# Where the value writes of a context projection stand in the DMA queue, and the last chunk's in two pieces

## The chip, the cores and the metric

The kernel runs on one core of one Trainium2 chip. The metric is device time in microseconds (us). Engines are named as the profile names them: PE is TensorE, DVE VectorE, ACT ScalarE, POOL GpSimd, SP SyncE, which here only issues DMAs and waits.

## What is computed

The reference is a four-layer Perceiver block stack. 128 latent tokens of width 256 attend, in each layer, to one context of 12544 tokens of width 192, with 16 heads of 16; then self-attention of some kind and a mixture of experts follow. Cut to what matters here:

```python
for l in range(4):
    x = x + cross_attention(layernorm(x), ctx_768, ...)   # q = x Wq; k = ctx Wk + bk; v = ctx Wv
    x = x + self_attention(layernorm(x))
    x = x + experts(layernorm(x))
```

The keys and values of layers 0, 1 and 2 depend on the context alone. They are computed once, in a first stage, and kept in DRAM.

## The kernel before

The stage in question is `project_context` (L190 to L397). Everything else in the kernel comes after it, behind a barrier of all engines, and is not touched.

The context comes transposed (192 x 12544) and is cut into 7 chunks of 1792 keys (`NCH`, `CH`), and each chunk into 2 halves of 896 (`W`), so 14 halves, i = 0 to 13. In half i the kernel makes, for 3 layers and 2 groups of 128 columns, six key tiles (n = 0 to 5), and seven value tiles (t = 0 to 6) of 128 keys x 768 columns.

- PE: `key_tile` (L273) and `value_tile` (L283) take turns, n = 0 to 5, then a seventh value tile. Both have two pairs of PSUM banks. A key tile waits until DVE has taken the key tile before the last, a value tile likewise (`values`).
- ACT: for each key tile `high` (L304) makes the first bf16 part, with a wait for the landing of the part six tiles back (`RING` = 6, semaphores `parts_out`), and `middle` (L311) the second part of the tile before. At the end of half i comes `round_context(i + 2)` (L315), which waits for the load of half i+2 (`ctx`).
- DVE: `key_rest` (L362) and `take_value` (L372) in turns, and at the half's end `low_context(i + 2)`. `take_value` copies a value tile into one of two buffers `values[c % 2]`, 128 x 48 x 14 x 17 fp32 (3 layers x 16 heads, 14 tiles of 128 keys, 16 values and a one). With the first tile of a chunk c it waits for the value writes of chunk c-2 (`values_out`).
- POOL: the third bf16 part of each key tile (L395, semaphore `low`).
- SP: all DMAs go out from one written order (L227 to L269). For each half and each n it waits for `low` and writes the three parts of the key tile (L255, 672 KB); behind n = 1 it issues `load(i + 2)` (L228: one DMA of 448 KB and two of 224 KB). Behind n = 5 of every odd half it waits for the chunk's 14 value tiles and issues three value writes, one for each layer (L265, 1904 KB each, in rows of 14 x 17 x 4 = 952 bytes). At the end SP waits for all landings, and the stage ends.

Of the kernel before, what the change touches and what calls it, by code (L numbers as in the profile page):

```python
# [38 lines left out]
H = 16  # L39
# [5 lines left out]
NCH = NK // CH  # L45
TPC = CH // 128
SUB = CH // 4
GT = TPC // 2
GW = GT * 128
VW = HD + 1  # L50
# [6 lines left out]
class Stage:  # L57
# [5 lines left out]
    def sem(self, name):  # L63
        if name not in self.sems:
            self.sems[name] = self.nc.alloc_semaphore(f"{self.tag}_{name}")
        return self.sems[name]
# [37 lines left out]
def dram(ap, offset, pattern):  # L104

    return bass.AP(ap.tensor, offset, pattern)
# [83 lines left out]
def project_context(nc, g, a):  # L190

    NL = 3
    W = CH // 2
    NH = 2 * NCH
# [3 lines left out]
    with ExitStack() as ctx:  # L198
        st = Stage(nc, ctx, "proj")
        sem = st.sem  # L200
# [11 lines left out]
        values = [st.sb(f"values{i}", [128, NL * H, TPC, VW]) for i in range(2)]  # L212
# [13 lines left out]
        @block.sync  # L226
        def _(sp):  # L227
            def load(i):  # L228
                keys = slice(i * W, i * W + W)
                if i >= 2:  # L230
                    sp.wait_ge(sem("split"), 2 * (i - 1))
                sp.dma_start(raw_a[i % 2][:], a["ctxT"][0:128, keys]).then_inc(sem(f"ctx{i % 2}"), 16)
                for copy in range(2):
                    sp.dma_start(raw_b[i % 2][copy * C1:copy * C1 + C1, :], a["ctxT"][128:C, keys])\
                      .then_inc(sem(f"ctx{i % 2}"), 16)

            for l in range(NL):
                cols = slice(l * D, l * D + D)
                for w, name in ((0, "Wk"), (1, "Wv")):
                    src = a[f"L{l}_xattn_{name}"]  # L240
                    sp.dma_start(w_a[:, w, cols], src[0:128, :]).then_inc(sem("weights"), 16)
                    for copy in range(2):
                        sp.dma_start(w_b[copy * C1:copy * C1 + C1, w, cols], src[128:C, :]).then_inc(sem("weights"), 16)
                if l > 0:
                    for k in range(DG):
                        sp.dma_start(bk[:, l, k:k + 1], dram(a[f"L{l}_xattn_bk"], 128 * k, [[1, 128], [1, 1]]))\
                          .then_inc(sem("weights"), 16)
            load(0)
            load(1)
            for i in range(NH):  # L250
                for n in range(NK2):
                    l, k, u = n // DG, n % DG, i * NK2 + n
                    sp.wait_ge(sem("low"), u + 1)
                    dst = dram(g.key_parts, ((l * 3) * D + k * 128) * NK + i * W, [[NK, 128], [D * NK, 3], [1, W]])
                    sp.dma_start(dst, parts[u % RING][:]).then_inc(sem(f"parts_out{u % RING}"), 16)  # L255
                    if n == 1 and i + 2 < NH:
                        load(i + 2)
                if i % 2 == 1:
                    c = i // 2
                    sp.wait_ge(sem("values"), TPC * (c + 1))  # L260
                    for l in range(NL):
                        dst = dram(g.values, l * g.layer_values + c * 128 * TPC * VW,
                                   [[TPC * VW, 128], [NCH * 128 * TPC * VW, H], [1, TPC * VW]])
                        src = values[c % 2][:, l * H:l * H + H, :, :].rearrange("p h t e -> p h (t e)")
                        sp.dma_start(dst, src).then_inc(sem(f"values_out{c % 2}"), 16)  # L265
            for r in range(RING):
                sp.wait_ge(sem(f"parts_out{r}"), 16 * len(range(r, NH * NK2, RING)))
            for r in range(2):
                sp.wait_ge(sem(f"values_out{r}"), 16 * NL * len(range(r, NCH, 2)))  # L269

        @block.tensor
        def _(pe):
# [2603 lines left out]
```

## Time and profile before

| | us |
|---|---|
| median of 3 runs | 3386.88 |
| the runs | 3374.2 to 3387.84 |
| the profiled execution | 3375.52 |
| its span | 3373.8 |
| the projection, start to last landing of its DMAs | about 467 |
| PE busy in the span | 2941.7 (87%) |
| value writes in the projection | 21, 1904 KB each, 17.4 us from issue to landing (median) |
| writes of key parts | 84, 672 KB each, 4.1 us (median) |

The profile is one execution. Its times count from the span's start. "SPq" is SP's sequencer issuing a DMA: the number there is the time that the issue took, not the transfer. A landing is counted from the start of the issue.

### The profile page before, as it was taken

What the parts mean: (1) busy time and instruction counts of PE and PEld (TensorE: products, weight loads), DVE (VectorE), ACT (ScalarE), POOL (GpSimd) and SP (SyncE); (2) the same over time, 40 slices, a digit from 0 to 9 for tenths busy, and PEclk for the clock granted to TensorE, in tenths of its full rate; (3) what the DMA queues carried; (4) which work ended last, traced back from release to release, by engine and by line L of the source; (5) the groups of instructions that cost most, each with busy time, mean ns of one, the idle gap of its engine ahead of it and who ended that gap; (6) DMA issues with size and microseconds to landing.
All of it is one profiled execution on the core that took longest, in us unless ns stands there. A gap on an engine that the chain in (4) does not pass through costs nothing. (4 is left out here: it accounts for less than half of the span.)

```text
span 3373.8 us, 66493 instructions
## 1 busy us (share of the span) xinstructions
PE 2941.7 (87%) x27158; PEld 2484.3 (74%) x27158; DVE 1829.3 (54%) x3246; ACT 1349.5 (40%) x2191; POOL 405.4 (12%) x571
## 2 busy tenths in 40 slices
PE   6878829998677999576999669999999999999978
PEld 6878725776474777473777455999999999999867
DVE  5445427774426775455776343555555555555524
ACT  4444314666003667122667120444344344444311
POOL 2333310000100000000000002220202020200000
PEclk9989968999787999686999685999999999999969
DMA  4877868883468884059885271201101010000016
GB/s 154 266 259 253 274 190 184 177 175 62 154 192 179 174 177 88 26 204 181 177 175 103 83 213 38 57 11 29 39 1 39 1 39 1 1 1 1 17 50 227
DMA packets 244901, 393.95 MB, mean 117 GB/s; under 512 B 33491, under 2 KB 207957, under 8 KB 244597
## 3 DMA queue, kind: packets, MB, share of 16 engines
q1 hardware_dynamic: 244599, 389.70, 44.9%
q8 instruction: 217, 3.56, 0.5%
q14 instruction: 85, 0.69, 0.1%
HBM read 289.45 MB, written 99.49 MB: 115 GB/s over the span
## 5 line engine op out<-in xcount | busy, mean ns | idle before, releaser
L697 DVE TENSOR_REDUCE L_xattn_tops<-psum 128x1 f32<-128x896 f32 x672 | 702.1, 1086 | 264.8 <-PE psum L549 263.6
L610 ACT ACTIVATE L_xattn_probs<-psum 128x512 f32<-128x512 f32 x1176 | 612.0, 600 | 489.4 <-PE psum L560 489.3
L1705 DVE TENSOR_TENSOR L_units_low<-psum,L_units_high 128x896 fp32r<-128x896 f32 x224 | 243.6, 1088 | 486.7 <-ACT L_units_high L1654 486.7
L549 PE MATMUL psum<-L_xattn_keys,L_xattn_q_stack 96*128 96x448 bf16 (+1 forms) x1344 | 393.6, 377 | 109.0 <-DMA L_xattn_q_stack<-query_parts 64.5
L1622 PE MATMUL psum<-wide_tokens,L_units_high 128*128 128x386 f32 x1568 | 456.4, 358 | 1.4 <-DVE L_units_low L1705 1.4
L560 PEld LDWEIGHTS psum<-L_xattn_q_stack,L_xattn_keys 99*128 99x128 bf16 (+1 forms) x4704 | 321.4, 98 | 143.3 <-issue 17.4
L560 PE MATMUL psum<-L_xattn_q_stack,L_xattn_keys 99*128 99x128 bf16 (+1 forms) x4704 | 392.4, 221 | 5.0 <-ACT L_xattn_probs L610 5.0
L1623 PE MATMUL psum<-wide_tokens,L_units_low 128*128 128x194 f32 x1568 | 395.1, 252 | 0.0
L573 PE MATMUL psum<-L_xattn_probs,L_xattn_values 128*17 128x128 f32 x9408 | 357.1, 276 | 0.0
L1654 ACT CAST L_units_high<-psum 128x896 fp32r<-128x896 f32 x224 | 203.3, 908 | 363.6 <-PE psum L1610 363.6
L1646 ACT ACTIVATE L_units_raw<-L_units_raw,L_units_negmax 128x896 f32<-128x896 f32 x224 | 221.6, 1037 | 307.9 <-DVE L_units_negmax L1696 307.9
L1623 PEld LDWEIGHTS psum<-wide_tokens,L_units_low 128*128 128x128 f32 x1568 | 299.1, 191 | 1.7
L1622 PEld LDWEIGHTS psum<-wide_tokens,L_units_high 128*128 128x128 f32 x1568 | 294.9, 188 | 3.0 <-DVE L_units_low L1705 1.6
L573 PEld LDWEIGHTS psum<-L_xattn_probs,L_xattn_values 128*17 128x17 f32 x9408 | 260.1, 98 | 38.0 <-ACT L_xattn_probs L610 0.6
L1686 DVE TENSOR_SCALAR_CACHE_REDUCE L_units_raw<-psum 128x448 f32<-128x448 f32 x448 | 259.8, 617 | 4.0 <-POOL wide_acc L1665 2.6
L549 PEld LDWEIGHTS psum<-L_xattn_keys,L_xattn_q_stack 96*128 96x128 bf16 (+1 forms) x1344 | 91.4, 99 | 219.1 <-issue 67.1
L1610 PE MATMUL psum<-band,L_units_raw 128*128 128x128 f32 x1568 | 207.9, 272 | 2.0 <-ACT L_units_raw L1646 2.0
L395 POOL TENSOR_TENSOR proj_parts<-proj_rest,proj_parts 128x896 bf16<-128x896 f32 x84 | 161.6, 1925 | 280.0 <-ACT proj_parts L313 280.0
L1610 PEld LDWEIGHTS psum<-band,L_units_raw 128*128 128x128 f32 x1568 | 179.9, 140 | 10.3 <-ACT L_units_raw L1646 2.4
L1598 PE MATMUL psum<-wide_high_a,wide_q_high 128*128 128x448 f32 x448 | 184.5, 412 | 2.2 <-PEq L78 2.2
L2563 PE MATMUL psum<-xnT,L_ffn_w 128*128 128x128 f32 x1056 | 141.6, 292 | 27.3 <-DMA L_ffn_w<-in_L_ffn_W 14.0
L2563 PEld LDWEIGHTS psum<-xnT,L_ffn_w 128*128 128x128 f32 x1056 | 137.3, 206 | 36.0 <-issue 14.0
(436 smaller groups left out, 3990.3 us busy)
## 6 DMA issues: line engine op xcount, KB each, us to landing
key_parts<-proj_parts SPq DMA_DIRECT2D x84, 672.0 KB, 4.1
L_xattn_keys<-key_parts SPq DMA_DIRECT2D x144, 336.0 KB, 4.7
values_scratch<-proj_values SPq DMA_DIRECT2D x21, 1904.0 KB, 17.4
L_xattn_values<-values_scratch SPq DMA_DIRECT2D x144, 238.0 KB, 5.2
L_ffn_w<-in_L_ffn_W SPq DMA_DIRECT2D x32, 1024.0 KB, 6.9
L_xattn_keys<-key_parts SPq DMA_DIRECT2D x144, 224.0 KB, 5.0
L_xattn_keys<-key_parts SPq DMA_DIRECT2D x192, 112.0 KB, 5.0
L_ffn_w<-in_L_ffn_w SPq DMA_DIRECT2D x16, 1024.0 KB, 6.4
```

The costliest lines, as they stand in the source:

```text
L549: last = pe.matmul(top_slot(n)[:, s, :], q_stack[0:P1, h, :], keys[0:P1, v % RING, key:key + WIN // 2], start=True, stop=True)
L560: last = pe.matmul(score_bank(k)[:, i * 128:i * 128 + 128], keys[0:P2, u % RING, key:key + 128], q_stack[0:P2, u // NCH, :], start=True, s ...
L573: last = pe.matmul(sum_bank[row:row + VW, :], values[:, u % RING, t, :], probs[:, at:at + 128], start=(c * TPC + t < 4), stop=(c * TPC + t ...
L610: act.activation(group_probs(k), score_bank(k), ACT.Exp).then_inc(sem("probs"), 1)
L697: dve.tensor_reduce(tops[:, h % 2, 2 * c + w:2 * c + w + 1], top_slot(n), AX.XY, ALU.max)\
L1610: last = pe.transpose(turned_banks(gr)[:, t * 128:t * 128 + 128], raw[u % 2][:, key:key + 128], g.ident)
L1622: pe.matmul(out, high[gr][:, cols], rhs, start=(tile == 0), stop=False, skip_group_check=True)
L1623: last = pe.matmul(out[:, 0:C + 2], low[gr][:, cols], rhs[:, 0:C + 2], start=False, stop=(tile == TPC - 1), skip_group_check=True)
L1646: act.activation(half, half, ACT.Exp, bias=new).then_inc(sem("probs"), 1)
L1686: dve.tensor_scalar(raw[u % 2][:, s * SUB:s * SUB + width], bank(g, s % 2, 0, width), 0.0, None, ALU.add, ALU.max, accum_out=tops[:, h, s: ...
L1705: dve.tensor_tensor(low[gr][:], turned_banks(gr), high[gr][:], ALU.subtract).then_inc(sem("low"), 1)
L2563: last = pe.matmul(bank(g, 2 * slot + half, j * T, j * T + T), buf[par][:, k, col:col + 128], g.xnT[:, k, :], start=(k == 0), stop=(k == D ...
```

## The change

Three things, all on SP. The load of half i+2 is issued behind parts n = 0 instead of n = 1. The three value writes of a chunk aren't issued together behind its last parts any more, but one by one in the next chunk: layer 0's behind parts n = 3 of its even half, layer 2's behind n = 1 and layer 1's behind n = 4 of its odd half. And the values of the last chunk, which has no next one, are written in two pieces for each layer: the first seven tiles (those of half 12) behind parts n = 2, 3 and 5 of half 13, the others behind its end. A row of such a piece has 7 x 17 x 4 = 476 bytes. The count at the end grows by three DMAs.

```diff
+            def store_values(c, l):
+                sp.wait_ge(sem("values"), TPC * (c + 1))
+                dst = dram(g.values, l * g.layer_values + c * 128 * TPC * VW,
+                           [[TPC * VW, 128], [NCH * 128 * TPC * VW, H], [1, TPC * VW]])
+                src = values[c % 2][:, l * H:l * H + H, :, :].rearrange("p h t e -> p h (t e)")
+                sp.dma_start(dst, src).then_inc(sem(f"values_out{c % 2}"), 16)
+
+            def store_last(half, l):
+                c, tiles = NCH - 1, slice(half * GT, half * GT + GT)
+                sp.wait_ge(sem("values"), TPC * c + GT * (half + 1))
+                dst = dram(g.values, l * g.layer_values + c * 128 * TPC * VW + half * GT * VW,
+                           [[TPC * VW, 128], [NCH * 128 * TPC * VW, H], [1, GT * VW]])
+                src = values[c % 2][:, l * H:l * H + H, tiles, :].rearrange("p h t e -> p h (t e)")
+                sp.dma_start(dst, src).then_inc(sem(f"values_out{c % 2}"), 16)
...
-                    if n == 1 and i + 2 < NH:
+                    if n == 0 and i + 2 < NH:
                         load(i + 2)
-                if i % 2 == 1:
-                    c = i // 2
-                    sp.wait_ge(sem("values"), TPC * (c + 1))
-                    for l in range(NL):
-                        dst = dram(g.values, l * g.layer_values + c * 128 * TPC * VW,
-                                   [[TPC * VW, 128], [NCH * 128 * TPC * VW, H], [1, TPC * VW]])
-                        src = values[c % 2][:, l * H:l * H + H, :, :].rearrange("p h t e -> p h (t e)")
-                        sp.dma_start(dst, src).then_inc(sem(f"values_out{c % 2}"), 16)
+                    if i >= 2 and n == 3 + i % 2:
+                        store_values(i // 2 - 1, i % 2)
+                    if i >= 2 and i % 2 == 1 and n == 1:
+                        store_values(i // 2 - 1, 2)
+                    if i == NH - 1 and n in (2, 3, 5):
+                        store_last(0, (2, 3, 5).index(n))
+            for l in range(NL):
+                store_last(1, l)
...
             for r in range(2):
-                sp.wait_ge(sem(f"values_out{r}"), 16 * NL * len(range(r, NCH, 2)))
+                sp.wait_ge(sem(f"values_out{r}"), 16 * NL * (len(range(r, NCH, 2)) + (r == (NCH - 1) % 2)))
```

## Rows read from the trace of the kernel before

**Rows 1.** Stretches: each engine's busy us (x instructions), granted clock, DMA share, GB/s.
```profile
26.00:102.50 76.50, 76.09 (x391) 71.69 (x391) 44.87 (x46) 37.26 (x47) 32.11 (x17) 1.00 0.61 195
102.50:165.10 62.60, 52.01 (x260) 48.67 (x260) 30.39 (x31) 25.86 (x32) 23.14 (x13) 0.92 0.81 254
...
443.80:468.20 24.40, 0.00 (x0) 0.00 (x0) 0.00 (x0) 0.00 (x0) 0.00 (x0) 0.50 0.97 275
```
**Rows 2.** Waits, 25 to 450 us: us in total, times, longest.
```profile
PE psum L279 <- DVE proj_rest L367: 53.9, 6, 10.6
...
ACT proj_high_a L319 <- DMA proj_raw_b<-in_ctxT: 72.9, 6, 14.6
```
**Rows 3.** Timeline of SP, end of half 3: start, us of issuing, line, DMA.
```profile
146.87 10.75 SPq L265 DMA_DIRECT2D values_scratch<-proj_values  x3
157.67 7.65 SPq L255 DMA_DIRECT2D key_parts<-proj_parts  x2
165.37 1.61 SPq L232 DMA_DIRECT2D proj_raw_a<-in_ctxT  x1
```
**Rows 4.** Timeline of ACT: rounding of a context half, undisturbed and late.
```profile
77.70 0.95 ACT L319 ACTIVATE proj_high_a<-proj_raw_a 128x896 fp32r<-128x896 f32 x1 [1.72 <-PE psum L289]
...
178.06 0.95 ACT L319 ACTIVATE proj_high_a<-proj_raw_a 128x896 fp32r<-128x896 f32 x1 [14.61 <-DMA proj_raw_b<-in_ctxT]
```
**Rows 5.** Timeline of PE at first key tiles of halves; then one stretch.
```profile
77.64 0.67 PE L279 MATMUL psum<-proj_high_a,proj_wh_a 128*128 128x448 f32 x2
...
102.49 0.47 PE L279 MATMUL psum<-proj_high_a,proj_wh_a 128*128 128x448 f32 x1
...
120.83 0.74 PE L279 MATMUL psum<-proj_high_a,proj_wh_a 128*128 128x448 f32 x1 [10.49 <-DVE proj_rest L367]
...
411.91 0.47 PE L279 MATMUL psum<-proj_high_a,proj_wh_a 128*128 128x448 f32 x1
...
120.83:126.91 6.08, 6.08 (x20) 5.65 (x21) 3.63 (x4) 2.76 (x3) 2.44 (x3) 0.61 0.61 226
```
**Rows 6.** Timeline of SP in half 1: load, then parts from n=2.
```profile
67.01 1.74 SPq L232 DMA_DIRECT2D proj_raw_a<-in_ctxT  x1
...
70.39 13.81 SPq L255 DMA_DIRECT2D key_parts<-proj_parts  x4
```
**Rows 7.** Value writes of chunk 0 and chunk 6: ns of issuing, starts, landings.
```profile
L265 SPq DMA_DIRECT2D values_scratch<-proj_values x3: 487/3166/6771, 84.2 to 88.0; - x3
DMA to landing us min/median/max: 10.4/17.6/21.4
...
L265 SPq DMA_DIRECT2D values_scratch<-proj_values x3: 533/3160/7168, 443.8 to 447.6; - x3
DMA to landing us min/median/max: 10.6/16.4/19.6
```
**Rows 8.** Parts' writes: two in a row; one alone; that of 70.39.
```profile
L255 SPq DMA_DIRECT2D key_parts<-proj_parts x2: 1211/1212/1212, 412.6 to 413.9; - x2
...
DMA to landing us min/median/max: 10.7/10.9/11.2
...
L255 SPq DMA_DIRECT2D key_parts<-proj_parts x1: 372/372/372, 78.0 to 78.0; - x1
...
DMA to landing us min/median/max: 3.2/3.2/3.2
...
DMA to landing us min/median/max: 5.5/5.5/5.5
```
**Rows 9.** Timelines of DVE and PE, half 2: first value copy, value tile 2.
```profile
83.02 0.95 DVE L378 COPY proj_values<-psum 128x768 f32<-128x768 f32 x1
...
87.39 0.51 PE L289 MATMUL psum<-proj_wh_a,proj_high_a 128*128 128x384 f32 x2
```
**Rows 10.** DMA queue, 444.9 to 460 and 500 to 503.6: packets, MB, share.
```profile
q1 hardware_dynamic: 4745, 4.69, 107.0%
...
q1 hardware_dynamic: 786, 0.24, 27.9%
```

## The prediction

> **What bounds the kernel now.** I read the table of stretches first [rows 1]. It cuts the projection at the first key tile of each odd half. From 26 to 102.5 us TensorE (PE) is busy 76.1 of 76.5 us, so an undisturbed half is PE's own time. In the next stretch, one chunk, PE is busy 52.0 us of 62.6, and four more like it follow; after 443.8 us no engine works for 24.4 us while DMA is busy 0.97 of the time. So there are two losses: some 11 us of PE in each chunk, and a tail of DMA alone.
>
> The waits say what stands behind the first [rows 2]: PE waited 53.9 us in six places for DVE's key rest, which itself follows ACT's high part, and ACT 72.9 us in six places, the longest 14.6, for the DMA that loads the context. The order on SyncE (SP) explains it [rows 3]: in an odd half the three value writes are issued at its end (146.87 us, 10.75 us of issuing). The next parts follow at 157.67 and the load only at 165.37, behind 5.9 MB of values in the same queue. ACT starts on that load at 178.06 after 14.61 us idle [rows 4]. PE's key tiles give the price [rows 5]: undisturbed, half 2 starts at 77.64 and half 3 at 102.49, so 24.85 us per half and 49.7 per chunk (which puts half 1's start at 52.79). From 102.49 (half 3) to 411.91 (half 13) five chunks took 309.4 us instead of 248.5: 60.9 lost, 12.2 each. Of one, 10.49 us is idle PE. The rest is that the pair of key and value tile after it takes 6.08 us (120.83 to 126.91) instead of 3.8 (parts go out every 3.8: n=2 of half 1 at 70.39, n=4 at 78.0 [rows 6, 8]). The granted clock there was 0.61, so mostly the 1.2 GHz level [rows 5]. So the clock costs 1.7 (12.2 less 10.49) to 2.3 us (6.08 less 3.8) per place; I take 1.9.
>
> **The change, part by part.** *Load behind the parts of n=0, value writes away from in front of it.* No instruction is added; for each half the load goes one part (3.8 us) earlier, and it no longer queues behind three value writes. In an even half it is issued at 10.4 us after the half's first key tile (parts n=0 of half 1 at 52.79+10.0: n=2 went out at 70.39, less twice 3.8). The queue has then at most one value write ahead. It lands at 21.3 us (worked out below), and ACT, where nothing holds it, turns to it at 24.9 (77.70 for the half from 52.79 [rows 4, 5]). So the 12.2 us go. Cover: 3.6 us; if it fails, each us late is a us of PE.
>
> *One value write at a time.* Each chunk's three writes move into the next chunk: l=0 behind parts n=3 of the even half, l=2 behind n=1 and l=1 behind n=4 of the odd half. All are the same 1904 KB. SP's waits for value tiles now ask for copies of the half before, at least two key tiles old, so they hold up nothing queued behind them (parts and loads). The writes' cost on the DMA is in the landings [rows 7]: three issued at 84.24, 84.8 and 88.0 landed 10.4, 17.6 and 21.4 us later, that is at 94.7, 102.4, 109.4: 7.0 to 7.7 each in a row; in the tail 6.3 and 6.5. I take 7.2 in the middle. Parts in a row cost 1.7 (412.6+10.7 and 413.9+11.2 [rows 8]) and 3.2 from issue to landing alone, so about 1.3 behind the transfer. A load with the parts before it holds the queue some 6 us: the parts issued at 70.39, 3.4 us behind the load's start, landed 5.5 us later instead of 3.2 [rows 6, 8], so they began at 72.7, 5.9 after the parts of 66.6 had gone out. Per chunk that is 12x1.7 + 3x7.2 + 2x4 = 50 us of DMA in 49.7 of PE: the queue only just keeps up.
>
> *The wait that this tightens.* DVE's first value copy of a new chunk c waits for the writes of chunk c-2, since there are two buffers. Before, these were out a whole chunk earlier and nobody waited. Now the last of them, l=1, is issued behind parts n=4 of the odd half just before. Parts n=4 of half 1 went out at 78.0 [rows 8], 0.35 us after half 2 had begun on PE (77.64), so the issue stands at 0.8 after that start. Ahead in the queue, in time from the odd half's first parts: load done 6.3, parts n=1 8.0, l=2 15.2, parts n=2 and n=3 18.6, parts n=4 20.3, l=1 27.5, landed 28.8. (Behind it parts n=5, the new half's parts n=0 and its load at 4 us end the transfer at 34.9, landed 36.2, which is the 21.3 above.) The new half begins at 14.85 (24.85 less 10.0), so the landing is at 13.95 in it, and the copy (0.95 us) ends at 14.9. Undisturbed it started at 83.02, 5.4 after the half's start [rows 9], so DVE stands still from then, and behind it in its order the key rest of n=1, for which ACT, GpSimd and the parts' writes wait in turn. PE has two PSUM pairs for values, so it goes on until value tile 2, at 87.39, 9.75 into the half [rows 9]. It then waits 5.1 us, and with the clock's 1.9 us that is 7.0. With an empty queue ahead it would land at 0.8+10.4 = 11.2, PE would wait 2.4 us and lose 4.3: the lower end. The upper end is 11.2, if what is ahead takes 4.2 us more; even with both writes at the slowest spacing of the rows, 7.7, it would be 1.0 more, so this end leaves room for SP being held by a full queue. I take 7.0, near the middle, five times: halves 4, 6, 8, 10 and 12. Halves 0 and 2 wait for nothing. The high part's wait on the ring of six parts doesn't bind: it has 24.85-10.0+2.0 = 16.9 us from issue to reuse, and the parts worst off, n=5 behind l=1, need about 9.
>
> So half 13 begins at 102.49 + 248.5 + 35.0 = 386.0 instead of 411.9.
>
> *The last chunk in two pieces.* Three writes of the first seven tiles go behind parts n=2, 3 and 5 of half 13, three of the others behind its end. Rows of the same 16x128 pieces shrink from 952 to 476 B: six writes of 2048 packets for three. The trace shows no write of this size. Its neighbours [rows 10]: 4745 packets of 4.69 MB, nearly all of 952 B, at 15.1 us x 1.07 x 16 = 54 ns each; 786 packets, nearly all of 256 B and written to DRAM, at 3.6 us x 0.28 x 16 / 786 = 20.5 ns. Between them 476 B is 31 ns, so a piece takes 2048 x 31 / 16 = 4.0 us. The ends: 3.5, half of a write, and 7.0, as long as a whole one because packets count and not bytes. I take 4.0, since the 256-B row shows that small packets are cheaper.
> The Trainium skill ("DMA: Bandwidth & Descriptors", Specifications) speaks against this edit: it gives 512 B as the least transfer for line rate, and says that below it the DMA engine reads, modifies and writes. Taken as every short packet going twice, a piece would be 8.0 us and the time 3391.7. The 256-B writes at 20.5 ns show nothing of it.
>
> The end, from half 13's first parts at 396.0 (10.0 behind its key tile): l=2 of chunk 5 moves from 5.5 to 12.7, parts 14.4, piece 18.4, parts 20.1, piece 24.1, parts 25.8, l=1 33.0, parts 34.7, four pieces 50.7, landed 52.0: 448.0 us. Before, the last landing was 447.6+19.6 = 467.2 [rows 7]; what follows it stays. Note that the tail behind half 13's start grows from 55.3 to 62.0 us, because two whole writes of chunk 5 now lie in it: the split saves less than this costs.
>
> Sum: 467.2 - 448.0 = 19.2 us. The profiled execution took 3375.5 us (span 3373.8), which would become 3356.3. The median of the runs is 3386.9, 0.3% above it, and the same 19.2 off gives **3367.7**.
>
> **The rivals.** *A, hardly a new wait.* If the queue is emptier than I count (value writes at the tail's 6.3 us, loads at 3.5), the value copy loses 4.3 us per chunk: 13.5 more, 3354. For it: the tail's landings [rows 7]. Against: all middle ones are 7.0 and over.
> *B, short rows are dear.* Pieces take 7 to 8 us: 18 to 24 more in the tail, 3386 to 3392, no change. For it: no row of this size, and packets of 256 B cost 20.5 ns, more than their share of bytes (256/952 of 54 is 14.5). The skill's rule above is of this kind.
> *C, slower: the value copy becomes the bound.* Place: the first value copy of chunks 2 to 6. The price is a us of PE per us of later landing, five times. It decides for no gain at 7.0+19.2/5 = 10.8 us lost per chunk, and for over 0.5% slower (17 us) at 14.2, that is a landing at 21.2 into the half instead of 13.95. At 16 us each: 3386.9 - 19.2 + 45 = 3413. For it: the queue has 50 us of work per 49.7, and SP is held when it is full (7.65 us for two parts at 157.67, where a free one takes 0.4 [rows 3, 8]), so backlog could carry over. Against: the wait itself stretches the chunk to 56.7 and lets the queue run empty.
> *D, the change doesn't do what it says.* The load comes late all the same, behind l=1, in even halves: 4 us in five of them bring 3388. For it: the 3.6 us of cover are thin. Against: up to 7 more from the stall itself.
>
> **How the numbers follow.** Forecast 0.48, A 0.17, B 0.20, C 0.08, D 0.07. The likeliest time is 3367.7. Range: A's 3354, less 3 for pieces at 3.5 us and 2 for scatter, 3349; above, B's and D's 3391. Outside it are C and extremes of A. A measurement of this kernel tells some 0.5% (17 us) from no change; my sum lies just beyond it. Faster by over that: A whole and 0.37 of the forecast's 0.48, 0.54. Within: the rest of the forecast, B and most of D, 0.36. Slower: C and B's worst, 0.10.
>
> **What would show it.** Right: ACT's waits for the context load gone (but for the start's); DVE's value copy waiting for value writes five times, 8 us each; PE's waits five times about 5 us; half 13 starting near 386; last landing near 448. Wrong: no wait of the value copy (A), pieces landing 7 us or more apart at the end (B), the copy waiting 12 us or more (C), ACT still waiting for a load (D).

## The result

| | before | after |
|---|---|---|
| median of 20 runs, us | 3386.85 | 3375.7 |
| lowest of them | 3374.2 | 3368.5 |
| profiled execution | 3375.52 | 3372.62 |
| half 13 starts on PE | 411.9 | 384.8 |
| last landing of the projection | 467.2 | 457.0 |
| from half 13's start to there | 55.3 | 72.2 |

The ratio is 0.9974, with a 95% interval of 0.9964 to 0.9984: 8.8 us less (5.4 to 12.2), 0.26%. It goes by the means; the medians lie 11.2 us apart. One of the 20 executions of the kernel before took 13405 us and is left out of it. I had forecast 19.2 us. The change helps, but with less than half of what I gave it by the ratio, and by the measure of 0.5% it counts as no difference.

The profiled executions differ by only 2.9 us although the projection ended 10.1 us earlier. The kernel before had been profiled in one of its quickest executions, 11 us under its median, and the stages behind the projection, whose code is the same, scatter: from the last landing of the projection to the end of the span it was 2906.6 us in the kernel before and 2913.9 in the changed one, and it lies between 2906.6 and 2917.0 in the twelve profiles of this study that have no probe in them. So for the parts of the sum I read the projection alone.

First the stretches of the changed kernel, with the columns of [rows 1]: halves 3 to 12, then half 13, then the tail.

```profile
103.13:384.84 281.71, 258.16 (x1301) 242.49 (x1301) 152.38 (x151) 130.41 (x160) 114.63 (x61) 0.96 0.87 280
...
384.84:409.60 24.76, 24.76 (x130) 23.40 (x130) 13.03 (x13) 11.95 (x13) 11.33 (x7) 1.00 0.93 287
409.60:457.00 47.40, 0.03 (x1) 0.00 (x0) 1.05 (x2) 0.00 (x0) 2.24 (x2) 0.53 1.13 210
```

The five chunks take 281.7 us, not 309.4. The tail behind PE's work is 47.4 us, where it was 24.4 [rows 1], and DMA moves only 210 GB/s in it, at a share of 1.13, where it moved 275. The waits of the changed kernel, where [rows 2] had PE on DVE's key rest and ACT on the load:

```profile
PE psum L304 <- DVE proj_values L393: 23.0, 5, 5.2
...
DVE proj_values L393 <- DMA values_scratch<-proj_values: 39.9, 5, 8.7
...
ACT proj_high_a L334 <- DMA proj_raw_b<-in_ctxT: 1.1, 1, 1.1
```

ACT's waits for the load are gone but for the start's 1.1 us. In their place DVE waits five times, 8.0 us on average, for the landing of a value write, and PE five times, 4.6 us on average, for DVE. One such place, half 4, in the timelines of SP, DVE and PE (compare [rows 3] and [rows 9]):

```profile
128.74 0.53 SPq L242 DMA_DIRECT2D values_scratch<-proj_values  x1
134.16 4.19 SPq L270 DMA_DIRECT2D key_parts<-proj_parts  x2
138.39 0.54 SPq L232 DMA_DIRECT2D proj_raw_a<-in_ctxT  x1
...
141.66 0.96 DVE L393 COPY proj_values<-psum 128x768 f32<-128x768 f32 x1 [8.22 <-DMA values_scratch<-proj_values]
...
142.68 0.83 PE L304 MATMUL psum<-proj_wh_a,proj_high_a 128*128 128x384 f32 x2 [4.79 <-DVE proj_values L393]
```

Layer 1's write goes out at 128.74, 0.8 us behind half 4's start (127.98); it lands at 141.64, DVE copies at 141.66, and PE's value tile 2 starts at 142.68. This is the wait of the prediction, in its place. The granted clock in the 3.3 us behind it is 0.53, the 1.2 GHz level:

```profile
142.68:146.00 3.32, 3.32 (x11) 3.32 (x12) 2.92 (x3) 0.94 (x1) 1.27 (x1) 0.53 0.78 224
```

The end of half 13, SP's timeline, and the pieces' landings (their issue line is L250):

```profile
399.05 0.49 SPq L242 DMA_DIRECT2D values_scratch<-proj_values  x1
402.43 0.75 SPq L270 DMA_DIRECT2D key_parts<-proj_parts  x1
403.23 1.34 SPq L250 DMA_DIRECT2D values_scratch<-proj_values  x1
...
417.71 0.60 SPq L242 DMA_DIRECT2D values_scratch<-proj_values  x1
418.36 6.49 SPq L270 DMA_DIRECT2D key_parts<-proj_parts  x1
424.90 20.38 SPq L250 DMA_DIRECT2D values_scratch<-proj_values  x4
...
L250 SPq DMA_DIRECT2D values_scratch<-proj_values x1: 5874/5874/5874, 439.4 to 439.4; - x1
DMA to landing us min/median/max: 17.6/17.6/17.6
...
q1 hardware_dynamic: 4787, 2.26, 108.8%
```

The last line is the DMA queue from 441 to 456.5 us, with the columns of [rows 10]: nothing but pieces. 15.5 us x 1.088 x 16 / 4787 = 56 ns for a packet of 476 B. I had put 31. A packet of twice the bytes took 54 [rows 10]. The 56 ns belong to the second pieces. Over all 12288 packets of 476 B in this trace the mean is 50.5 ns: about 43 for the three pieces of the first seven tiles, 58 for the three of the others.

### The profile page after: what moved, and what is told of

It is laid out like the page before. It is cut to its first block and busy times, and to the rows that moved or that the text cites. A ratio compares the mean times of both kernels' runs of the same rounds, so it can differ in the third digit from the quotient of the medians.

```text
span 3370.9 us, 66496 instructions
## 1 busy us (share of the span) xinstructions
PE 2945.2 (87%) x27158; PEld 2487.7 (74%) x27158; DVE 1830.0 (54%) x3246; ACT 1350.9 (40%) x2191; POOL 404.1 (12%) x571
## 5 line engine op out<-in xcount | busy, mean ns | idle before, releaser
L1637 PE MATMUL psum<-wide_tokens,L_units_high 128*128 128x386 f32 x1568 | 456.5, 358 | 1.4 <-DVE L_units_low L1720 1.4
L575 PEld LDWEIGHTS psum<-L_xattn_q_stack,L_xattn_keys 99*128 99x128 bf16 (+1 forms) x4704 | 323.1, 98 | 144.4 <-issue 19.2
L2578 PE MATMUL psum<-xnT,L_ffn_w 128*128 128x128 f32 x1056 | 141.3, 292 | 27.5 <-DMA L_ffn_w<-in_L_ffn_W 14.2
L2578 PEld LDWEIGHTS psum<-xnT,L_ffn_w 128*128 128x128 f32 x1056 | 137.3, 206 | 35.8 <-issue 14.2
```

The costliest lines, as they stand in the source:

```text
L575: last = pe.matmul(score_bank(k)[:, i * 128:i * 128 + 128], keys[0:P2, u % RING, key:key + 128], q_stack[0:P2, u // NCH, :], start=True, s ...
L1637: pe.matmul(out, high[gr][:, cols], rhs, start=(tile == 0), stop=False, skip_group_check=True)
L2578: last = pe.matmul(bank(g, 2 * slot + half, j * T, j * T + T), buf[par][:, k, col:col + 128], g.xnT[:, k, :], start=(k == 0), stop=(k == D ...
```

## Experiments

They ran in four series, each on a chip of its own (named A to D), and in each against the kernel before. On A and B its projection is to be seen at the start of the two probe kernels below: half 13 at 421.9 and 424.3, the last value write landed at 481.6 and 482.0 us, 14 to 15 later than in the first pair. The medians of the kernel before are only 6 to 8 us higher in the series (3392.6 to 3394.4) than in the first pair, and the first pair's profile lies 11 us under its median, so how much of the 14 to 15 us is the chip and how much the single execution stays open. The changed kernel was therefore run again, on B and on D. "Last landing" is that of the projection, in one profiled execution. A difference between two kernels is sure in the projection only within a series, or where it is well above the one to three us by which the repeated ones differ (466.3 and 467.8, 419.4 and 422.0). Each profile is one execution.

| kernel | chip | half 13 starts | last landing | ratio to before (95%) |
|---|---|---|---|---|
| before | A, B | 421.9, 424.3 | 481.6, 482.0 | |
| changed, again | B | 390.8 | 466.3 | 0.9974 (0.9962 to 0.9985) |
| changed, again | D | 391.7 | 467.8 | 0.9972 (0.9957 to 0.9986) |
| changed, last chunk whole | A | 390.6 | 450.5 | 0.9913 (0.9889 to 0.9938) |
| before, with pieces | A | 422.2 | 492.1 | 1.0048 (1.0030 to 1.0066) |
| before, load behind n=0 | B | 418.9 | 476.6 | 0.9989 (0.9972 to 1.0005) |
| changed, rows and pieces aligned | C | 359.4 | 419.4 | 0.9836 (0.9819 to 0.9852) |
| the same, again | D | 361.7 | 422.0 | 0.9830 (0.9812 to 0.9848) |
| early writes, pieces | C | 352.2 | 421.7 | 0.9834 (0.9818 to 0.9851) |
| early writes, last chunk whole | A | 351.7 | 404.9 | 0.9776 (0.9749 to 0.9803) |
| the same, rows aligned | B | 352.1 | 400.1 | 0.9759 (0.9734 to 0.9785) |

> The changed kernel itself, beside the others of this series. In the first series the kernel before had its projection end at 481.6 us, not at 467.2, with half 13 starting at 421.9, not 411.9; so DMA is slower there, and the changed kernel has to be seen under the same conditions. Expected from e1_whole_last (450.5 for the last landing) plus 6 to 12 us for the pieces: last landing 457 to 463, 0.3 to 0.6% faster than before.

The last landing, 466.3, is later than that, and the 0.26% are under it: the pieces cost more than the 6 to 12 us that I gave them here.

**The pieces taken back out of the change.**

```diff
-                    if i == NH - 1 and n in (2, 3, 5):
-                        store_last(0, (2, 3, 5).index(n))
-            for l in range(NL):
-                store_last(1, l)
+            for l in range(NL):
+                store_values(NCH - 1, l)
```

> The changed kernel, with the last chunk's values written whole: three writes of 1904 KB behind the end of half 13, no pieces. Theory 1 (rows of 476 B are dear by themselves: 5.6 us a piece in the changed kernel's tail, where a whole write of twice the bytes takes about 6.9): half 13 starts at 385 as there, its parts follow from 398.6-3.8; from there 12.7 + 5 parts' 1.7... to the end of layer 1's write of chunk 5 about 25, parts 26.7, three whole writes 20.7, landing 1.3: last landing near 444 to 447 instead of 457.0, so 10 to 13 us faster than the changed kernel, some 20 faster than before. Theory 2 (pieces cost 4.0 us as forecast, and the tail was long because SP was held behind a full queue, 5 to 7 us an issue): whole writes fill the queue as much, last landing 452 to 458, no gain over the changed kernel.

Half 13 starts where it did (390.6), and the last landing is at 450.5. My two theories were worked out for a half 13 that starts at 385. With the 5.8 us by which it starts later here, theory 1 (dear rows) gives 450 to 453 and theory 2 (SP held) 458 to 464. Against the changed kernel it is 15.8 to 17.3 us earlier, across chips on which half 13 starts alike (390.6, 390.8, 391.7), and the ratios, each against before beside it, lie apart: about 0.6% of the whole kernel. SP is held just as long, 7.4 us for the last issue:

```profile
L242 SPq DMA_DIRECT2D values_scratch<-proj_values x1: 7387/7387/7387, 429.0 to 429.0; - x1
DMA to landing us min/median/max: 21.5/21.5/21.5
```

So it isn't SP's hold. The split gave back some two thirds of what the rest of the change had gained (0.87% without it, 0.26% with it).

**The pieces put alone into the kernel before.**

```diff
+                    if i == NH - 1 and n in (2, 3, 5):
+                        store_last(0, (2, 3, 5).index(n))
-                if i % 2 == 1:
+                if i % 2 == 1 and i < NH - 1:
...
+            for l in range(NL):
+                store_last(1, l)
```

> The kernel before with one part of the change alone: the last chunk's values in two pieces for each layer, at the places of the change (behind parts n=2, 3 and 5 of half 13, and behind the end). Loads and all other writes as before. Work in the queue from the parts of n=2 (433.95 before): four parts at 1.7 and six pieces. Theory 1 (5.6 us a piece): 434 + 6.8 + 33.6 + 1.3 = 475.7 instead of 467.2, 8 us slower in the stage. Theory 2 (4.0 a piece): 434 + 6.8 + 24 + 1.3 = 466.1, 1 us faster.

Half 13 starts as in the kernel before; the last landing is 492.1, 10 us later than the 481.6 to 482.0 there. The whole kernel is 0.5% slower (0.3 to 0.7). Theory 1 had 8, theory 2 a gain of 1.

**The load's place alone.**

```diff
-                    if n == 1 and i + 2 < NH:
+                    if n == 0 and i + 2 < NH:
```

> The kernel before with the load of half i+2 behind the parts of n=0 instead of n=1, nothing else. Theory (the three value writes ahead of it in the queue are the delay, and SP's hold, not the place among the parts): the load goes out when the third value write has been taken in, 102 instead of 103.4 us, and lands 1.5 to 3 us earlier; the chunk's stall falls from 12.2 to 9.5 to 10.7; stage 7 to 13 us shorter. Rival (the place of the load is most of the change's gain): stall under 6 us, stage over 25 us shorter.

The last landing is 5 us earlier in single executions, less than I expected, and the ratio's interval holds 1, so no gain is shown. ACT still waits for the load, as long as before ([rows 2] had 72.9, longest 14.6):

```profile
ACT proj_high_a L319 <- DMA proj_raw_b<-in_ctxT: 75.5, 6, 15.8
```

So the load's place alone doesn't free it. The other part of the change, the value writes no longer standing in front of it, must have; that part alone, with the load left behind n=1, was not run.

**A probe for the price of a row.** Behind the projection's last landing the kernel before writes groups of three from a value buffer to scratch DRAM, 2048 rows each, and waits for each group.

```diff
+            for k, (tiles, pitch) in enumerate(probe_rows):
+                for m in range(3):
+                    n = tiles * VW
...
+                    sp.dma_start(dst, src).then_inc(sem("probe"), 16)
+                sp.wait_ge(sem("probe"), 48 * (k + 1))
```

> The kernel before with a probe behind the projection's last landing: seven groups of three writes from a value buffer to scratch DRAM, 2048 rows each, each group awaited before the next. Rows: 952 B at a pitch of 952; 476 B at 952; 476 B at 512; 544 B at 952; 408 B at 952; and the first two again. Nothing of it enters the output. Time of one write is the spacing of landings in a group. Cost by bytes and packets alone (my forecast's line, 20.5 ns at 256 B, 54 at 952): 6.9, 4.0, 4.0, 4.4, 3.6 us. Rows below 512 B are dear (read-modify-write): 476 and 408 B both about 5.6 or more and dearer than 544 B. Partial lines are dear, whatever the length: 476 B at a pitch of 952 about 5.6, at a pitch of 512 about 4, and 544 B dear too.

> The kernel before with a second probe behind the projection: groups of three writes of 2048 rows, each group awaited. Row and pitch in bytes: 952/952 is known (6.7 us by spacing). 952/960, 952/1024, 476/480, 476/512, 476/1024, 476/1024 starting 476 B in, 512/512. If the start's alignment decides: 952/1024 clearly under 6.7, 476/512 and 476/1024 near 3.7, 476/1024 starting at 476 near 6, 512/512 near 4; the pitches of 960 and 480 tell how coarse the grid is (64 or 32 B would do, or not). If it is the pitch or neighbouring rows sharing a line, the group that starts at 476 with a pitch of 1024 is as cheap as the one that starts at 0.

Time of a group, from its first issue to its last landing (the third write's start and the longest landing, less the first's start):

| row, pitch, first byte | first probe, us | second probe, us |
|---|---|---|
| 952, 952, 0 | 22.4 and 21.9 | 22.6 |
| 476, 952, 0 | 20.6 and 20.7 | |
| 544, 952, 0 | 18.9 | |
| 408, 952, 0 | 18.0 | |
| 952, 960, 0 | | 19.2 |
| 952, 1024, 0 | | 18.9 |
| 476, 480, 0 | | 14.4 |
| 476, 512, 0 | 13.1 | 13.5 |
| 476, 1024, 0 | | 13.4 |
| 476, 1024, 476 | | 22.6 |
| 512, 512, 0 | | 12.3 |

Four of these groups as the trace has them (first and second of 476 B are of the first probe, at pitches of 952 and 512; the others of the second, at a pitch of 1024, starting at 0 and 476 B in):

```profile
L277 SPq DMA_DIRECT2D probe_scratch<-proj_values x3: 360/1621/5114, 504.1 to 506.1; - x3
DMA to landing us min/median/max: 8.3/15.2/18.6
...
L277 SPq DMA_DIRECT2D probe_scratch<-proj_values x3: 360/1849/3525, 524.7 to 527.0; - x3
DMA to landing us min/median/max: 5.6/9.1/10.8
```

```profile
L275 SPq DMA_DIRECT2D probe_scratch<-proj_values x3: 360/1834/3538, 570.8 to 573.1; - x3
DMA to landing us min/median/max: 6.1/9.2/11.1
...
L275 SPq DMA_DIRECT2D probe_scratch<-proj_values x3: 359/1732/6564, 584.2 to 586.4; - x3
DMA to landing us min/median/max: 10.2/16.9/20.4
```

The same 476 B in the same 2048 rows take 13.4 us a group when each row starts on a multiple of 1024 B and 22.6 when each starts 476 B behind one. The source, the pitch and the length are the same in both, so the difference is the row's start in DRAM; a packet took 26.7 ns in the one group and 60.1 in the other. A pitch of 480, a multiple of 32, costs 14.4, nearly as little, although its rows cross multiples of 256 and 512 B like those at 952; so crossing them isn't what is dear. Starts on multiples of 32 B give nearly all of it; a finer grid wasn't tried. Rows of 408 B at a pitch of 952 cost 18.0, of 544 B 18.9, of 952 B 22: along this line there is no step at 512 B. The Trainium skill ("DMA: Bandwidth & Descriptors", Specifications) puts a read-modify-write below 512 B. These groups show no such limit by length: aligned rows of 476 B cost 13.1 to 13.5 beside 12.3 for 512 B, and whole rows of 952 B cost a fifth more at their own pitch (22.6) than at 1024 (18.9).

Something smaller is left over. Rows of 476 B cost a little more than longer ones at either kind of start (20.6 beside 18.9 for 544 B, 13.1 to 13.5 beside 12.3 for 512 B). 476 isn't a multiple of 8 B and the other lengths are; whether the row's end is the reason was not tried. What happens inside the DMA engine or the memory on such a start was not looked at.

**The alignment inside the kernel.** The change as it is, with value rows at a pitch of 256 floats and pieces of 8 and 6 tiles.

```diff
+ROW = 256
...
-                c, tiles = NCH - 1, slice(half * GT, half * GT + GT)
+                c, tiles, many = NCH - 1, slice(half * 8, 8 + half * 6), 8 - half * 2
...
-                           [[TPC * VW, 128], [NCH * 128 * TPC * VW, H], [1, GT * VW]])
+                           [[ROW, 128], [NCH * 128 * ROW, H], [1, many * VW]])
```

> The changed kernel in its own order of writes, with every value row beginning at a multiple of 1024 B in DRAM and the last chunk's pieces made of 8 and 6 tiles (544 and 408 B) instead of 7 and 7, so that the second piece begins 544 B in, a multiple of 32 B. Same bytes, same number of packets, same places. Theory (the start off a 32-B grid is what cost the forecast its 1.6 us a piece): a piece takes about 4 us (4.3 and 3.7), so the six take 24 instead of 35 us; whole writes take 5.7 instead of 6.7, so DVE's value copy is released 2 us earlier five times and half 13 starts 8 to 12 us earlier than the 390.8 of e5_changed_again; last landing 441 to 448 instead of 466.3; 0.5 to 0.8% under the changed kernel. Rival (short rows are dear in themselves, or SP's hold is the limit): pieces stay at 5.5 to 6 us, last landing over 452.

The last piece of four lands 11.4 us behind its issue at 408.0, so at 419.4; the first went out at 396.7 and landed at 407.3:

```profile
L251 SPq DMA_DIRECT2D values_scratch<-proj_values x1: 1340/1340/1340, 396.7 to 396.7; - x1
DMA to landing us min/median/max: 10.6/10.6/10.6
...
L251 SPq DMA_DIRECT2D values_scratch<-proj_values x1: 3187/3187/3187, 408.0 to 408.0; - x1
DMA to landing us min/median/max: 11.4/11.4/11.4
```

The last three, of 408 B, took 12.1 us, 4.0 each, and all six 24.8 us, 4.1 each. That is the forecast's 4.0 us in size. But these pieces differ from the change's in length as well as in start, so the probe has to say which counts more: the start gave 7 to 9 us a group, the lengths of 544 and 408 B instead of 476 at most 2.7. And half 13 starts 31 us earlier than in the changed kernel on B, not 8 to 12, because the faster whole writes take the wait with them:

```profile
PE psum L305 <- DVE proj_values L394: 5.8, 5, 1.6
...
DVE proj_values L394 <- DMA values_scratch<-proj_values: 22.8, 5, 4.8
```

The changed kernel on B had:

```profile
PE psum L304 <- DVE proj_values L393: 27.9, 5, 6.7
```

I had expected 2 us off each wait; PE's went from 27.9 us in all to 5.8, 4.4 off each. The remaining 9 of the 31 us are the clock's share: its granted mean over halves 3 to 12 is 1.00, where it was 0.94.

The two kernels stood on different chips, so both ran once more on D.

> The changed kernel once more, on one chip with the kernel of aligned rows and pieces, since the two stood in different series. If the difference seen between the series is the alignment's: six pieces again 5.5 to 6 us each, PE's five waits 23 to 28 us in all, half 13 at 385 to 391, ratio to before 0.996 to 0.9985. If it was the chip's, half 13 and the last landing here come near those of the aligned kernel beside it.

> The changed kernel with aligned rows (pitch 1024 B) and pieces of 8 and 6 tiles, beside the changed kernel on one chip. If it is the alignment: pieces 4.0 us each, PE's five waits 5 to 7 us in all, half 13 at 357 to 361, last landing 417 to 421 and 45 us before the other's; ratio 0.982 to 0.985. If the chip: the two differ by less than 20 us in the projection.

The waits of PE in the changed kernel, then in the aligned one:

```profile
PE psum L304 <- DVE proj_values L393: 28.5, 5, 6.8
```

```profile
PE psum L305 <- DVE proj_values L394: 7.1, 5, 1.9
```

Half 13 at 391.7 against 361.7, the last landing at 467.8 against 422.0: 45.8 us between the two on one chip, and 1.4% of the kernel's time. It is the alignment, not the chip. (Half 13's start and PE's waits in both, and the last landing of the aligned one, lie up to 1 us outside the bounds that I had set.) The 30 us up to half 13 come from the whole rows' alignment alone, since no piece has been written by then.

**The writes placed earlier.** From the change without pieces, one more edit:

```diff
-                    if i >= 2 and n == 3 + i % 2:
+                    if i >= 2 and n == 1:
                         store_values(i // 2 - 1, i % 2)
-                    if i >= 2 and i % 2 == 1 and n == 1:
+                    if i >= 2 and i % 2 == 0 and n == 4:
                         store_values(i // 2 - 1, 2)
```

> As e1_whole_last, and the value writes of a chunk stand earlier in the next one: behind parts n=1 and n=4 of the even half and n=1 of the odd one, instead of n=3 of the even and n=1 and n=4 of the odd. My theory of the wait: the last write of chunk c-2 then lands 45.1 us behind the even half's first parts, where DVE asks for it at 45.1 and PE would miss it at 48.5, so the five stalls of PE (3.7 to 5.3 us, and the clock behind them) go: half 13 starts at 351 to 358 instead of 385, last landing near 405 to 415 instead of 457; 42 to 50 us faster than the changed kernel, 1.3 to 1.5%. Rival: the queue has 50 us of work per 49.7 us chunk and becomes the bound; loads land late (ACT waits for them) and half 13 starts at 365 or later, stage end 425 or later.

```profile
103.19:152.90 49.71, 49.59 (x261) 46.82 (x261) 30.46 (x31) 25.97 (x32) 22.87 (x13) 1.00 1.03 321
302.02:351.72 49.70, 49.59 (x260) 46.81 (x260) 30.45 (x31) 25.97 (x32) 22.85 (x13) 1.00 0.98 313
```

These are halves 3 and 4, and halves 11 and 12. PE is busy 49.6 of 49.7 us in both, the clock is full, and neither DVE nor PE waits for a value write. DMA moves 313 to 321 GB/s beside it. The queue I feared (50 us of work per chunk) is full but doesn't hold PE or DVE up. Half 13 starts at 351.7, at the early end of the forecast; the time is 2.2% under the kernel before and clearly under the changed one.

> e4_early_writes with the last chunk in the change's pieces (476 B, places as in the change) instead of whole. With no stall in front of it, the queue behind half 13's parts of n=1 is: layer 1's write, four parts, six pieces. From 375.7, where that write ends in e4_early_writes: 4x1.7 + 6x5.8 + 1.3 gives a last landing near 418 instead of 404.9, 13 us or 0.4% more. If the pieces cost 4.0 us, 408 and 3 us.

With the pieces put back (on C) the last landing is 421.7 instead of 404.9 (on A), 17 us later, and the time 0.6% higher: the pieces cost the same in either order.

> e4_early_writes with one more change: each row of 952 B in DRAM begins at a multiple of 1024 B (pitch 256 floats instead of 238); writes and reads keep their 952 B. Theory (a start off the DRAM's grid is what makes a packet dear; the probe had 476 B at a pitch of 512 at 3.7 us and at 952 at 6.2): value writes fall from 6.7 to 5.5 us or less, the last three end some 3 to 4 us earlier, and the reads of values in the three streamed attentions (69 ns a packet in the mean over the kernel before) get cheaper, which shows only where those stages wait for DMA. Rival (952 B is long enough, only short packets are dear): spacing of the last three unchanged at 6.5 to 7, time within 3 us of e4_early_writes.

Aligned rows in the fastest order: the last three writes land 9.0, 14.2 and 16.6 us behind issues at 379.5 to 383.5, so 5.8 apart instead of 6.9, and the projection ends 4.8 us earlier. The intervals of the two ratios overlap. The reads in the later stages show no gain: behind the projection it is 2910.6 us here and 2908.8 with unaligned rows, well inside the scatter. (The 69 ns a packet in the expectation are the mean of the projection from 26 to 468.2 us, not of the whole kernel or of those reads.) Of the kernels here this one has the lowest time, 3311.7 us beside 3393.2 before.

## Why the prediction was right and wrong

**The stalls that go, right.** ACT no longer waits for a load. The 60.9 us of five chunks [rows 5] were there to be had: with early writes halves 3 to 12 took 248.5 us (103.2 to 351.7), the undisturbed time.

**The wait that takes their place, right in place and size.** Five times, 8.0 us for DVE (forecast: some 8), 4.6 us for PE (forecast 5.1), the clock behind it; half 13 at 384.8 (forecast 386.0). The working from the queue's order held to about a microsecond: layer 1's write was to land 13.95 us into the half, and did at 13.7 (141.64 less 127.98), and the five waits with the clock cost 33.2 us (281.7 less 248.5), where I had 35.0. That it fits so closely is in part luck: on B and on D the same kernel lost 39.4 and 39.7 us there, with waits of 5.6 and 5.7 us for PE. All of this is inside the ends that I gave (4.3 to 11.2 per chunk).

**The pieces, wrong, and this is the step that failed.** From half 13's start I summed 62.0 us; it took 72.2. The term in front of the pieces holds: layer 2's write of chunk 5 landed 24.9 us behind half 13's start (409.7), where I had 24.0. The term "2048 x 31 / 16 = 4.0" should have been near 5.9: from the landing of parts n=2 (402.4 + 8.3 = 410.7) to the last one (457.0) are 46.3 us, less 6.8 for layer 1's write and 3.9 for three parts leaves 35.6 for six pieces, 11.6 more than I gave them (these shares go by the spacing of the landings). The other terms behind layer 2's write came out 2.3 us shorter than summed, which makes the 10.2 us. The 4.0 came from a line between 256-B packets at 20.5 ns and 952-B packets at 54 ns. The 256-B rows (query parts, at a pitch of 256) start on the grid and the 952-B rows start off it three times out of four, so the two ends of the line differed in two things, and I took all of the difference for length. "Grid" here means multiples of 32 B, which were enough in the probe. The pieces start off the grid more often still: the first one's rows at multiples of 952 B, one in four on a multiple of 32, the second one's, 476 B on, never. The probe gives the four prices apart, per group of three: 13.4 and 22.6 for 476 B, 18.9 and 22.4 for 952 B. In it two aligned 476-B writes land 3.3 to 4.1 us apart, about what I had for a piece.
My upper end for a piece was 7.0, and rival B stood at 7 to 8 us: its direction was right and its size too high. I had named the Trainium skill's read-modify-write below 512 B ("DMA: Bandwidth & Descriptors", Specifications) as of its kind; neither the probe nor the kernel with aligned pieces (408 B, 4.0 us each) shows a packet going twice for being short.

**The note that the tail grows, right, and not acted on.** I wrote that the split saves less than the two whole writes of chunk 5 cost. In fact it saves nothing: without it the changed kernel's projection ends some 16 us earlier, and even at 4.0 us a piece six of them are 24 us of queue where three whole writes are 20.

**The whole time.** Projection: 10.1 us gained in the first pair, 19.2 forecast; on B 15.7, in single executions on both sides. Kernel: 8.8 us (5.4 to 12.2). That B shows more in the projection and the same 0.26% in the time stays open; the later stages' scatter (2906.6 to 2917.0 us) is enough for it, but was not followed. The first pair's 10.1 us may be too little, since its kernel before was profiled in a quick execution.

## What to carry to other kernels

When a transfer is moved out of another's way, work out from the queue's order when it will land now and who waits for that: here the new wait ate half of the gain (33.2 of 60.9 us), and three key tiles earlier for the last write did away with it. Give rows that are written to DRAM a start on a multiple of 32 B (14.4 us a group at a pitch of 480 B, 20.6 at 952), and when a price is interpolated between two sizes, look whether they differ in anything else. Pieces that double the packets of a queue which is already the bound must be cheaper than half each to pay, and these were not.

## What the hardware showed unexpectedly

Writes to DRAM of 476-B rows cost 13.4 us per three DMAs when rows start on 1024 B, 14.4 at a pitch of 480 B, 22.6 when all start 476 B behind a multiple of 1024; 952-B rows 18.9 against 22.4. In the kernel with early writes and pieces DMA moved 320 GB/s at a share of 1.01 from 103.6 to 352.2 us, and PE was busy for 247.9 of these 248.5 us. And the projection of the same kernel before ended 14 us apart (467.2 and 481.6 to 482.0) in single executions on different chips; whether by the chip or the execution is not shown.
